# Swin block and masked MLP block on one core: another way to choose six tokens in order

## What is computed

```python
scores = jnp.einsum('gbcl,gc->gbl', xb, conv_w)
e = jnp.exp(scores)
p = e / jnp.sum(e, axis=-1, keepdims=True)
_, idx = jax.lax.top_k(p, K)
mask = jnp.sum(jax.nn.one_hot(idx, L, dtype=p.dtype), axis=2)
st = jax.lax.stop_gradient(mask - p) + p
out = st[:, :, None, :] * xb
idx_s = jnp.sort(idx, axis=-1)
gath = jnp.take_along_axis(out, idx_s[:, :, None, :], axis=-1)
feat = jnp.concatenate([gath.transpose(0, 1, 3, 2).reshape(NB, n, K * c), st], axis=-1)
h = jax.nn.relu(feat @ W1 + b1)
rec = (h @ W2 + b2).reshape(NB, n, OC, LH, LW)
...
return jnp.einsum('bohw,co->bchw', grid, out_w)
```

## Time and profile before

| | us |
|---|---|
| runs of the kernel, three | 783.03, 784.10, 784.84 |
| median | 784.1 |
| span of the profiled execution, first to last instruction | 778.6 |
| time of the profiled execution beside its span | not given apart |
| mean granted PE clock in it | 0.923 of full speed |
| last stage, where the change lies | 677.8 to 778.6 of the span |
| choice of tokens in it (first MAX8 to last one-hot row) | 681.0 to 692.1 |

### The profile page before, as it was taken

How to read it: one execution, slowest core, us unless ns; L and a number is a source line. 1 busy time by engine, 2 the same in 40 slices (tenths; PEclk the granted TensorE clock), 3 DMA queues, 4 the chain that set the end, 5 groups by cost and what they waited for, 6 DMA issues and landing times. The chain is left out here.

```text
span 778.6 us, 21192 instructions
## 1 busy us (share of the span) xinstructions
PE 665.7 (86%) x8584; PEld 371.4 (48%) x8584; DVE 516.4 (66%) x997; ACT 480.4 (62%) x963; POOL 355.1 (46%) x441
## 2 busy tenths in 40 slices
PE   4785789999999999999998579999999988749880
PEld 2562455565565555655555232233333367735350
DVE  4796487877777787877778322577777786372181
ACT  3565266777777777777775548877777656624000
POOL 4696446778777777788776520022221123100000
PEclk9787599999999999999999959999999999969955
DMA  9550000000000000000000020122112220120278
GB/s 216 137 128 11 1 3 2 3 2 3 2 3 3 3 3 3 3 2 3 3 2 3 2 56 1 28 55 56 33 50 55 55 55 2 31 72 2 63 194 269
DMA packets 15719, 31.44 MB, mean 40 GB/s; under 512 B 7488, under 2 KB 9284, under 8 KB 15620
## 3 DMA queue, kind: packets, MB, share of 16 engines
q1 hardware_dynamic: 12592, 29.16, 14.1%
q10 hardware_dynamic: 2760, 0.66, 0.5%
q0 software_dynamic: 272, 0.27, 0.2%
HBM read 20.71 MB, written 9.37 MB: 39 GB/s over the span
## 5 line engine op out<-in xcount | busy, mean ns | idle before, releaser
L794 POOL TENSOR_TENSOR sc<-sc,mx 128x512 f32<-128x512 f32 x128 | 133.7, 1044 | 102.4 <-DVE mx L725 102.4
L722 DVE TENSOR_TENSOR sc<-s_ps,bias_tab 128x512 f32<-128x512 f32 x128 | 87.7, 685 | 52.6 <-PE s_ps L528 52.6
L1424 POOL TENSOR_TENSOR square<-xs 128x1024 f32<-128x1024 f32 x16 | 34.1, 2133 | 165.5 <-DVE xs L1166 165.5
L539 PE MATMUL t_ps<-consts,sc 128*128 128x128 f32 x512 | 84.4, 288 | 16.2 <-ACT pt L656 12.5
L656 ACT ACTIVATE pt<-t_ps 128x512 f32<-128x512 f32 x128 | 75.7, 592 | 31.2 <-PE t_ps L539 30.1
L539 PEld LDWEIGHTS t_ps<-consts,sc 128*128 128x128 f32 x512 | 54.3, 142 | 84.8 <-issue 48.1
L725 DVE TENSOR_REDUCE mx<-sc 128x8 f32<-128x512 f32 x128 | 87.8, 686 | 4.4
L1081 ACT ACTIVATE hs<-h_ps,fb1s 128x512 f32<-128x512 f32 x128 | 78.2, 689 | 19.1 <-PE h_ps L990 19.0
L528 PE MATMUL s_ps<-kx,qu 32*64 32x128 f32 x2048 | 72.3, 278 | 3.5 <-DVE kx L749 2.9
L990 PE MATMUL h_ps<-xs,fw 64*128 64x512 f32 x256 | 68.7, 650 | 1.0 <-ACT hs L1081 1.0
L528 PEld LDWEIGHTS s_ps<-kx,qu 32*64 32x64 f32 x2048 | 56.7, 134 | 15.2 <-issue 13.4
(11 more groups left out here) (207 smaller groups left out, 1295.2 us busy)
## 6 DMA issues: line engine op xcount, KB each, us to landing
raw<-in_x_dram SPq DMA_DIRECT2D x32, 256.0 KB, 5.1
xr<-in_x_dram SPq DMA_DIRECT2D x32, 256.0 KB, 3.9
out_dram<-x SPq DMA_DIRECT2D x32, 256.0 KB, 3.9
rec_scratch<-r SPq DMA_DIRECT2D x4, 224.0 KB, 2.5
w<-in_L_conv_W_dram SPq DMA_DIRECT2D x1, 784.0 KB
w<-in_L_conv_W_dram SPq DMA_DIRECT2D x1, 672.0 KB
xs<-rec_scratch SPq DMA_DIRECT2D x16, 28.0 KB
xs<-rec_scratch ACTq DMA_DIRECT2D x16, 28.0 KB
```

The lines of the kernel that those rows point to most:

```text
L539: last = pe.transpose(t_ps[:, m], sc[n % KEPT][:, m].rearrange("c h k -> c (h k)"), ident)
L722: dve.tensor_tensor(sc[n % KEPT][:, :, :, :], s_ps[j][:, :, :, :], bias_tab[:, j, hp], ALU.add)\
L794: pool.tensor_tensor(v, v, mx[n % KEPT][:, :].unsqueeze(2).broadcast_to([128, 8, TOK]), ALU.subtract)\
```

## The change

The six places are negated and sorted by one more MAX8 per row group, so that they come in ascending order at once: `tidf` (filled with -64 beforehand, so that its last two entries are the smallest) takes the first six places times -1, and MAX8 of its eight entries gives `ordered`. `iota` holds 0 to -63. One compare over 128 x 6 x 256 makes the one-hot rows in order. The values `kept` = (1 - `pr`) + `pr` are computed for every place, and the one-hot rows are multiplied by them in two halves of three rows (128x768 each). The scan, the product with `cm` and the second compare are gone. PE starts with the first half of the rows as soon as it is multiplied, so its four rounds are reordered (half by half instead of row group by row group). `st`, the sum over the six, is made behind DVE's pick copies, transposed by PE in the third round of gathers, and copied by DVE behind its third feature copy. `N_PICK` is 11 instead of 13.

```diff
--- before.py
+++ after.py
@@ -1498,18 +1498,17 @@
 
         with ExitStack() as stage:
             s = {k: sem(stage, "t_" + k) for k in (
-                "own", "rows", "exped", "pick", "picked_t", "picked_a", "picked_b", "st_t", "st_copied", "gathered",
+                "own", "rows", "exped", "pick", "state", "picked_t", "picked_a", "picked_b", "st_t", "st_copied", "gathered",
                 "gathered_copied", "feat_ps", "feat_a", "feat_b", "hid_ps", "hid", "rec_ps", "rec", "mixed",
                 "added", "stored")}
             rec_out = [sem(stage, f"rec_out{h}") for h in range(2)]
             rec_in = [sem(stage, f"rec_in{h}") for h in range(2)]
             e = sb(stage, "e", [128, 4, TOK])
-            pr, st, cm = (sb(stage, n, [128, 4, TOK]) for n in ("pr", "st", "cm"))
+            pr, st, kept = (sb(stage, n, [128, 4, TOK]) for n in ("pr", "st", "kept"))
             esum = sb(stage, "esum", [128, 4])
             top = sb(stage, "top", [128, 4, 8])
             tidx = sb(stage, "tidx", [128, 4, 8], U32)
-            tidf = sb(stage, "tidf", [128, 4, 8])
-            zeros = sb(stage, "zeros", [128, TOK])
+            tidf, ordered = (sb(stage, n, [128, 4, 8]) for n in ("tidf", "ordered"))
             sel = sb(stage, "sel", [128, TOP, 4, TOK])
             picked = [sb(stage, f"picked{k}", [128, 4, 128]) for k in range(2)]
 
@@ -1592,7 +1591,7 @@
                     for b, (lo, hi) in enumerate(HALVES):
                         last = dve.tensor_copy(scores[lo:hi], yt[lo:hi, :, :, :, C + b])
                     last.then_inc(s["own"], 1)
-                    dve.memset(zeros[:, :], 0.0)
+                    dve.memset(tidf[:, :, :], -TOK)
                     dve.wait_ge(iota_in, 16)
                     dve.wait_ge(s["exped"], 2)
                     full = [128, 4, TOK]
@@ -1604,42 +1603,39 @@
                     link(last)
                     for t in range(4):
                         last = dve.max_index(tidx[:, t], top[:, t], pr[:, t])
+                    dve.tensor_scalar(kept[:, :, :], pr[:, :, :], -1.0, 1.0, ALU.mult, ALU.add)
                     link(last)
-                    link(dve.tensor_copy(tidf[:, :, :], tidx[:, :, :]))
-
-                    for k in range(TOP):
-                        last = dve.tensor_tensor(sel[:, k], iota[:, :].unsqueeze(1).broadcast_to(full),
-                                                 tidf[:, :, k:k + 1].broadcast_to(full), ALU.is_equal)
+                    link(dve.tensor_scalar(tidf[:, :, 0:TOP], tidx[:, :, 0:TOP], -1.0, None, ALU.mult))
+
+                    for t in range(4):
+                        last = dve.max(ordered[:, t], tidf[:, t])
                     link(last)
-                    link(dve.tensor_reduce(st[:, :, :].rearrange("c t l -> c (t l)"),
-                                           sel[:, :, :, :].rearrange("c k t l -> c (t l) k"), X, ALU.add))
-
-                    for t in range(4):
-                        last = dve.tensor_tensor_scan(cm[:, t], st[:, t], zeros[:, :], 0.0, ALU.add, ALU.add)
-                    link(last)
-                    link(dve.tensor_tensor(cm[:, :, :], cm[:, :, :], st[:, :, :], ALU.mult))
-                    link(dve.tensor_tensor(st[:, :, :], st[:, :, :], pr[:, :, :], ALU.subtract))
-                    link(dve.tensor_tensor(st[:, :, :], st[:, :, :], pr[:, :, :], ALU.add))
-                    for k in range(TOP):
-                        last = dve.scalar_tensor_tensor(sel[:, k].rearrange("c t l -> c (t l)"),
-                                                        cm[:, :, :].rearrange("c t l -> c (t l)"), float(k + 1),
-                                                        st[:, :, :].rearrange("c t l -> c (t l)"),
-                                                        ALU.is_equal, ALU.mult)
-                    link(last)
+                    link(dve.tensor_tensor(kept[:, :, :], kept[:, :, :], pr[:, :, :], ALU.add))
+                    every = [128, TOP, 4, TOK]
+                    link(dve.tensor_tensor(sel[:, :, :, :], iota[:, :].unsqueeze(1).unsqueeze(1).broadcast_to(every),
+                                           ordered[:, :, 0:TOP].rearrange("c t k -> c k t").unsqueeze(3)
+                                           .broadcast_to(every), ALU.is_equal))
+                    for half in range(2):
+                        part = sel[:, 3 * half:3 * half + 3].rearrange("c k t l -> c k (t l)")
+                        link(dve.tensor_tensor(part, part, kept[:, :, :].rearrange("c t l -> c (t l)").unsqueeze(1)
+                                               .broadcast_to([128, 3, 4 * TOK]), ALU.mult))
                     assert links[0] == N_PICK
-
                     dve.wait_ge(tail_zero, 2)
                     for n in range(4):
                         dve.wait_ge(s["picked_t"], n + 1)
-                        spread_picks(dve.tensor_copy, n, n // 2, n % 2, 0).then_inc(s["picked_a"], 1)
-                    dve.wait_ge(s["st_t"], 1)
-                    for b, (lo, hi) in enumerate(HALVES):
-                        last = dve.tensor_copy(st_t[lo:hi].rearrange("c a (n b) -> c a n b", b=2)[:, :, :, b],
-                                               psb[2][lo:hi, 0:256].rearrange("c (n a) -> c a n", a=2))
-                    last.then_inc(s["st_copied"], 1)
+                        spread_picks(dve.tensor_copy, n, n % 2, n // 2, 0).then_inc(s["picked_a"], 1)
+                    dve.tensor_reduce(st[:, :, :].rearrange("c t l -> c (t l)"),
+                                      sel[:, :, :, :].rearrange("c k t l -> c (t l) k"), X, ALU.add)\
+                       .then_inc(s["state"], 1)
                     for n in range(8):
                         dve.wait_ge(s["feat_ps"], n + 1)
                         spread_feat(dve.tensor_copy, n, 0).then_inc(s["feat_a"], 1)
+                        if n == 2:
+                            dve.wait_ge(s["st_t"], 1)
+                            for b, (lo, hi) in enumerate(HALVES):
+                                last = dve.tensor_copy(st_t[lo:hi].rearrange("c a (n b) -> c a n b", b=2)[:, :, :, b],
+                                                       psb[2][lo:hi, 0:256].rearrange("c (n a) -> c a n", a=2))
+                            last.then_inc(s["st_copied"], 1)
                     dve.wait_ge(tail_in, 16 * len(tail_loads))
                     for i, t in enumerate(ROW_TILES):
                         dve.wait_ge(s["rec_ps"], i + 1)
@@ -1665,7 +1661,7 @@
                     act.wait_ge(tail_zero, 2)
                     for n in range(4):
                         act.wait_ge(s["picked_t"], n + 1)
-                        spread_picks(copy, n, n // 2, n % 2, 1).then_inc(s["picked_b"], 1)
+                        spread_picks(copy, n, n % 2, n // 2, 1).then_inc(s["picked_b"], 1)
 
                     def spread(n):
                         act.wait_ge(s["feat_ps"], n + 1)
@@ -1691,10 +1687,10 @@
                     for t in range(2):
                         pe.transpose(psb[t][:, 0:128], scores[:, 8 * t:8 * t + 8].rearrange("c p g a -> c (p g a)"),
                                      ident).then_inc(s["rows"], 1)
-                    pe.wait_ge(s["pick"], N_PICK)
                     pe.wait_ge(s["exped"], 2)
                     for n in range(4):
-                        t, half = n // 2, n % 2
+                        half, t = n // 2, n % 2
+                        pe.wait_ge(s["pick"], N_PICK - 1 + half)
                         after(pe, s["picked_a"], n - 1)
                         after(pe, s["picked_b"], n - 1)
                         for k in range(3):
@@ -1702,10 +1698,6 @@
                                                 sel[:, 3 * half + k, 2 * t:2 * t + 2].rearrange("c b l -> c (b l)"),
                                                 ident)
                         last.then_inc(s["picked_t"], 1)
-                    for t in range(2):
-                        last = pe.transpose(psb[2][:, 128 * t:128 * (t + 1)],
-                                            st[:, 2 * t:2 * t + 2].rearrange("c b l -> c (b l)"), ident)
-                    last.then_inc(s["st_t"], 1)
                     pe.wait_ge(s["picked_a"], 4)
                     pe.wait_ge(s["picked_b"], 4)
 
@@ -1729,6 +1721,12 @@
                     for n in range(1, 8):
                         gather(n)
                         turn_back(n - 1)
+                        if n == 2:
+                            pe.wait_ge(s["state"], 1)
+                            for t in range(2):
+                                last = pe.transpose(psb[2][:, 128 * t:128 * (t + 1)],
+                                                    st[:, 2 * t:2 * t + 2].rearrange("c b l -> c (b l)"), ident)
+                            last.then_inc(s["st_t"], 1)
                     turn_back(7)
                     pe.wait_ge(s["feat_a"], 8)
                     pe.wait_ge(s["feat_b"], 8)
@@ -1765,7 +1763,7 @@
                             mix(k, half)
 
 
-N_PICK = 13
```

(3 more changed lines are left out.)

## The result

| | median us | lowest to highest | runs |
|---|---|---|---|
| before | 783.14 | 781.91 to 784.84 | 7 |
| after | 778.4 | 773.68 to 781.54 | 7 |

The ratio of after to before is 0.9929, with a 95% interval of 0.9904 to 0.9954: 0.7% faster. Two later series with the same changed kernel gave 0.9947 (0.9920 to 0.9974) and 0.9934 (0.9912 to 0.9956).

The account below looks back on a forecast made before the run. In the last block, DVE's chain of small instructions for the choice was taken as the bound, PE waiting. Saved 5.57, less 0.29 for `st` transposes and 0.3 for the clock, gave 5.0 us: span 773.6, time 779.1, range 777.7 to 781.9.

Parts of the forecast that it names:

- the base: Starting time of the whole kernel before: 784.1 us, from three runs spread over 1.8, median moving some 0.5 either way.
- the lower bounds of the narrow operations: In the choice: `kept` at least 0.18 us instead of 0.29, four MAX8 at least 0.30 instead of 0.38.
- part 1: From the last index search to PE's first transpose of one-hot rows: 3.99 us instead of 9.56, 5.57 saved.
- part 2: Transposes and copies of picks before the gathers: taking the two `st` transposes out gains 0.
- part 3: Sum over the six, 2.74 us, moved behind DVE's last pick copy: covered by 0.06 before the first feature copy.
- part 4: PE's rounds of gathers: the two `st` transposes add 0.29 us; their DVE copies fit into its idle time.
- part 5: PE's granted clock around the gathers: a later rise from 1.2 GHz costs 0.3 us, ends 0 and 1.9.
- The prediction's own sign of being wrong: In the gathers: a granted clock of 0.50 for several microseconds would show the forecast wrong.
- rival (a): At the gathers the clock rises late, losing 1.9 to 3.8 us: 780.7 to 782.6, likeliest 781.3; chance 0.20.
- (c): Clock stays at 1.2 GHz through all eight gather rounds: 791.6 us; slower than before beyond 10.6 us; chance 0.03.
- What lies around the span: Time outside the profiled span of the kernel before: 784.1 - 778.6 = 5.5 us, left unchanged by the change.
- The case for which the prediction cited that section: At `kept` on DVE, GpSimd's memset of `r` shares a port: no cost; memset 0.3 us later, `kept` waits 0.2.

Follow-up runs that it names:

- six_compares: The changed kernel with six compares of 256 instead of one of 1,536; 777.58 us in one execution.
- one_product: The changed kernel with one product over 1,536 instead of two over 768, PE waiting for the whole; 783.90 us in one execution.
- reduce_first: The changed kernel with DVE's sum over the six back ahead of its pick copies; median 779.48 us, ratio 0.9959.
- warm_after: The changed kernel with 46 transposes of the identity filling PE's idle time during the choice; median 777.07 us, ratio 0.9938.
- before_again: The kernel before, profiled once more without an edit; 783.39 us in this one execution.
- pool_kept_warm: The changed kernel with 42 filling transposes on PE during the choice and the two operations for `kept` on GpSimd; median 776.77 us, ratio 0.9929.
- paced: The changed kernel with `kept` on GpSimd, PE filled in five bursts during the choice and by 28 transposes before the mixing; median 775.77 us, ratio 0.9934.

## Where the prediction was right, and which steps failed

The mechanism was right; two terms had the wrong size. The time came out 1.5 us below the forecast 779.1 (777.6). 1.0 of it is the base and 0.6 the gain, 5.6 us where 5.0 stood.

- **The base is the step that put the time outside the range.** The prediction took 784.1, the median of three runs, and allowed that it moves "by some 0.5 either way". Seven runs of the same kernel gave 783.14, which is 1.0 lower, and the later series 781.93 (35 runs), 782.08 (11), 782.23 (20) and 782.02 (11). The lower end of the range, 777.7, doesn't follow from what the prediction names for it either: the lower bounds of the narrow operations (0.11 and 0.08) and the 0.5 give 778.4. Single executions of the changed kernel run from 773.7 to 783.3.
- **The choice** (part 1) was forecast at 3.99 us from the end of the last index search to PE's start. In the changed kernel the search ends at 679.96 and PE starts at 684.04: 4.08. Item by item: `kept` with the copy of the places 0.31 for 0.35, narrow MAX8 0.41 for 0.41, `kept` + `pr` 0.46 for 0.45, compare 1.79 for 1.78, product to PE 1.11 for 1.00. The largest difference is the hand-over to PE, 0.14 instead of 0.04. Saved in the choice: 5.49 instead of 5.57. six_compares and one_product confirm the two differences of size inside it (0.34 and 0.80).
- **The picks** (part 2): 3.85 as forecast. That the transposes of `st` had held up nothing is right at half clock.
- **The reduction** (part 3): it ran 687.73 to 690.56 (2.83 for 2.74), and reduce_first prices its move at 2.5 us. The forecast cover of 0.06 us was so thin that it would have been a guess had PE needed the copy at once. In the profile it wasn't tested, since the late clock moved the first feature copy to 692.62; in warm_after the gathers and the transposes back ran at full speed and PE had no gap (rounds 14.00 = 13.78 + 0.22), so it holds there too.
- **The rounds** (part 4): 0.22 for the two transposes of `st` (chain, 694.18), forecast 0.29; the whole tail of `st_t` was covered.
- **The clock** (part 5) is the other term that was mis-sized, and the other way. It had an allowance of 0.3 us, read from one execution in which the rise came almost with the first gather; in the profiled pair it cost 2.1. The prediction's own sign of being wrong, a clock of 0.50 in the gathers for several microseconds, was there: 4.6 us of it. The first two gathers took 3.58, 3.04, 2.76, 2.90, 3.58 and 3.57 us in the six unfilled executions with the new choice, and 1.95 and 2.74 in the two of before, against 1.88 at full clock. By the rounds, the new kernel's executions lie 0.9 to 2.2 us above the 14.00 of warm_after, those of before 0.1 and 0.9 above 13.78. So rival (a), with a chance of 0.20, described the clock of the profiled execution and its loss (1.9 to 3.8), but not the time that it gave for it (780.7 to 782.6). Eight executions are too few to say that the change makes the rise later; it is as well possible that the first profile of before was only lucky. When the clock rises, and on what it depends, stays open. The slower side (c) needed 10.6 us at half clock, and none of these had more than 5.
- **What lies around the span.** I took 784.1 - 778.6 = 5.5 us for it. In every execution whose own time is known it is 1.7 to 2.0 (775.21 - 773.4 = 1.8 in after, 783.39 - 781.6 = 1.8 in before_again). So the execution whose trace I read took about 780.4 by this measure, less than any of the three times beside it, and most of the 5.5 was the difference between two executions. It did no harm, because the sum was a difference.
- **Partly luck.** From the first MAX8 to the hidden layer the profiled pair gained 28.80 - 25.61 = 3.2 us, and any pair of profiled executions of the two kernels, neither of them filled, between 3.2 and 5.2. The 5.0 of the forecast lies at the upper end of that, because its clock term was too small. The 5.6 of the first series is above even the 5.16 with the clock held; where the rest came from isn't shown.
- **The two rules.** The Trainium skill, page "VectorE: DVE Perf Modes", section "The perf-mode tier table (the rule you actually need)", has a reduction at one element a cycle. The traces don't agree: the reduction took 2.74 to 2.91 us in the fourteen executions for 1,536 inputs read with a long step, a compare of 1,536 took 1.76, and the measurement decides. The Trainium skill, page "SBUF — State Buffer", section "Who interferes with whom", also says that a VectorE instruction with two SBUF inputs contends with a GpSimd instruction that reads SBUF. pool_kept_warm agrees: 1.92 instead of 1.76 for the compare beside GpSimd's 0.73 us operation. The case for which the prediction cited that section, one of the two waiting for the other, did not arise in the change itself (`kept` took 0.27, so its 0.14 us of distance held) and showed in paced.

The forecast gain was 5.0 us. With the clock held the change is worth 5.16 (one execution of each kernel); the three series gave 0.71%, 0.53% and 0.66% of some 783, that is 5.6, 4.1 and 5.2 us.

## What to carry to other kernels

On a chain of small vector operations every step can be priced from its neighbours' rows to about a tenth of a microsecond: shorten it by ordering the data once (sort six numbers, not 64 flags), by one wide operation for six narrow ones, and by handing the first half on early; move a sum that feeds nothing soon behind what is waited for. When such a chain has another engine idle, the first work of that engine afterwards may run at its lower clock for a time that differs from execution to execution: don't price it from one trace, and compare stretches inside the stage, not spans. And don't take the base from three runs when the forecast is a time: here four more moved it by 1.0 us. To hold the clock by filling the idle engine, let the filling follow the chain (bursts behind its links), because the filling itself runs at either speed. That held the clock in the one profiled execution of it; a lower median than with one block of filling wasn't shown.

## What the runs showed of the hardware

- The rise and fall of the granted clock differ between executions of one and the same program. In the changed kernel it rose 4.6, 2.4 and, in the third execution, about 1.8 us after the first gather; up to the first transpose back the two gathers took 1.88 us at 2.4 GHz and 3.58 at 1.2 GHz, the three transposes 0.53 and 0.89 to 0.92.
- PE idle for 0.77 to 1.02 us between filling and picks kept the clock at 1.00 in three executions; with 2.40 and 2.45 us idle it was lost in the picks, in both. In paced the gaps were 0.53 us at most and the clock held. Lengths between 1.02 and 2.40 didn't occur.
- A reduction over six values that lie 1 KB apart takes 1.6 times as long as a two-tensor operation with as many inputs (2.83 against 1.76 us in the changed kernel), and beside it gathers at full clock are not slowed (1.95 with it, 1.95 without). The reduction took 2.74 to 2.76 us in the three executions in which PE stood idle beside all or most of it, and 2.82 to 2.91 in the eleven in which PE worked beside it; why isn't shown.
- What lies around a span was 1.7 to 2.0 us in each of the executions whose own time is known.
